# A delta-rule attention layer with a mixture of experts on one core: the 16-to-32 merge in 64x64 weights, and a new order of the work lists

## The chip, the cores and the metric

The kernel runs on one core of one Trainium2 chip. The metric is device time of one execution in microseconds (us), the median of the runs shown. A core has a matrix engine (PE, TensorE), a vector engine (DVE), a scalar engine (ACT), GpSimd (POOL) and a sync engine (SP) that only issues DMAs here. They work on 128 partitions of on-chip memory, each with its own instruction list, and meet at semaphores only.

## The reference, cut to what matters

```python
# x: (2, 2048, 128); 8 heads, key and value width 128
x = x + attention(layernorm(x))          # gated delta rule
x = x + moe(layernorm(x))                # 8 experts, the best 2 of each token

def step(S, inp):                        # inside attention, token by token
    q_t, k_t, v_t, beta_t, alpha_t = inp
    S = S * alpha_t
    kv = einsum('bhk,bhkv->bhv', k_t, S)
    S = S + einsum('bhk,bhv->bhkv', k_t, (v_t - kv) * beta_t)
    return S, einsum('bhk,bhkv->bhv', q_t, S)
```

q, k and v come from a projection and a causal convolution with four taps over time. The output is RMS-normalised per head, gated with silu(z), projected and added to x.

## The kernel before, in words

The 4096 tokens are 32 chunks of 128. Two chunks make a *group*; there are 16 groups. Inside a chunk the recurrence is solved with matrices: a lower triangular 128x128 matrix N per head and chunk (`Nm`) has to be turned into the inverse R of (1 + N), and then the chunk is a handful of 128x128 products.

The inverse is built bottom up. DVE inverts all 16x16 diagonal blocks by substitution (words `inv.0` to `inv.10`, lines 1055 to 1079; the blocks of a group lie one to a partition). They go out to DRAM (`to` on SP, `tp` on ACT) and come back as blocks on the diagonal of the 128x128 layout (`ti` on SP, line 508 for the tile `TA` and 511; `tj` on ACT, line 764). Then three merges double the block size. The first is the one that changes: `y16` (L1508) multiplies, for 16 head-chunks and 4 blocks of 32, a 32x32 weight of `Nm` by a 32x16 block of `TA`; ACT copies the result to `Y16` (`ye`, L807); `r16` (L1516) multiplies `Y16` by the other diagonal blocks; DVE negates the result into R (`re`, four instructions, L1209) and transposes the 32x32 blocks (`td`, L1218). The words `m.c.0` to `m.c.3` on PE with `me.c.0` to `me.c.3` on ACT are the merges to 64 and 128 (L1528 to L1564). After them `u.c.h` uses R.

All five lists come from one string, `ORDER`. Each engine walks the words from left to right and executes those that are its own; a word has a meaning in three pipelined stages: it *finishes* group g (merges, recurrence, output), it *prepares* group a = g+1 (projection, convolution, N, its inverse), and it *routes* the tokens of group g-1 to experts (words `sm s2 nr xt xe lg rk pf ps sc`). So the order of two words matters only where they are on the same engine. One pass over the string is called a period here. Words that come up below:

- 24 tiles of q, k and v: `proj.n` on PE (three matmuls, L1618 to L1620), `taps.n` on ACT (two instructions, L771), `first.n` on DVE (L1162, L1165), `last.n` on POOL (L650). The PSUM banks of `proj` are two: `proj.n` waits for `first.n-2`. The SBUF buffers are four: `taps.n` waits for `last.n-4`.
- `ka`, `aq` (POOL, L630), `diag` (POOL, L640), `scan` (DVE, L1173), `kk`, `kq`, `ktr` (PE, L1606, L1604), `nm`, `at` (DVE, L1183, L1193).
- `v`, `ks`, `u`, `sd`, `o` (PE, L1656, L1665, L1674, L1682, L1693), `rhs`, `ue`, `sq`, `kd` (ACT), `st`, `g`, `zg`, `x2` (DVE, L1225, L1236, L1199, L1243), `sp` (POOL, L662), `rms` (DVE), `gn`, `gte` (ACT, L856, L861), `gt`, `out` (PE, L1701, L1708).
- `rk`, `ps` (DVE) rank the experts and give each token a place; `sc` (POOL, L619) sends the rows of the group to their places with four indirect DMAs.

`y16` waits for the landing of all block DMAs (`t_in`). After the 16 groups the experts run over tiles of 256 rows; the diff does not touch that part.

## Time and profile before

| what | value |
|---|---|
| median of 3 runs | 1503.14 us (1501.5 to 1505.62) |
| profiled execution, its own time | 1506.71 us |
| its span, first to last instruction | 1504.6 us |
| PE busy, share of the span | 1171.7 us, 78% |
| PE weight loads | 1014.5 us, 67% |
| DVE | 1078.4 us, 72% |
| ACT | 926.1 us, 62% |
| POOL | 773.3 us, 51% |
| mean granted PE clock | 0.900 of full speed |
| chain of waits, share by engine | PE 37%, DVE 26%, issue 18%, ACT 8%, POOL 5% |

"Busy" is the time in which at least one instruction of the engine ran. "Issue" in the chain of waits is time in which an engine waited for nothing that the profile shows. A line of a timeline gives start, duration, engine, source line, operation, tiles, shape and count; in brackets the idle time of the engine before it and what ended it. A product of 32-bit numbers stands in the records as two MATMUL and two LDWEIGHTS, so 64 products of `y16` are 128 and 128 records. The first `y16` begins at 112.17 us, the last at 1202.23 us. The rest is the set-up before and the last group and the experts after.

### The profile page before, as it was taken

The numbers are of one execution on the slowest core, as the hardware profiler recorded it, in microseconds if no ns is written. First come the engines' busy times: TensorE is split into PE (matmuls) and PEld (weight loads), VectorE is DVE, ScalarE is ACT, GpSimd is POOL, SyncE is SP. The second block draws the span as 40 slices with busy tenths as digits, with TensorE's granted clock in tenths as the row PEclk, the third lists the DMA queues.
The fourth block names the chain that finished last, engine by engine and source line by source line (L and its number), as shares of the span: only waits on it lengthen the run. The fifth ranks groups of instructions, "written<-read, shape, count | busy, mean of one in ns | idle before, by whom it ended". The sixth has DMA issues, their size and how long they took to land.

```text
span 1504.6 us, 42594 instructions
## 1 busy us (share of the span) xinstructions
PE 1171.7 (78%) x15946; PEld 1014.5 (67%) x15946; DVE 1078.4 (72%) x2512; ACT 926.1 (62%) x2804; POOL 773.3 (51%) x723
## 2 busy tenths in 40 slices
PE   1478897979797979888888888888888875188881
PEld 1247786868686868777777777777877765176771
DVE  6686777777777777786868686868786914576664
ACT  1355775767576767676767676767575834166663
POOL 1237464646565565655555656474838332145452
PEclk9989998989798989898989999999998968599996
DMA  5132222221212121212121222222221241422214
GB/s 137 43 66 54 38 56 45 53 55 44 56 42 56 42 57 42 57 42 57 41 57 41 57 46 55 44 65 37 66 41 59 43 120 31 124 59 63 61 51 170
DMA packets 213501, 89.27 MB, mean 59 GB/s; under 512 B 167064, under 2 KB 200734, under 8 KB 212405
## 3 DMA queue, kind: packets, MB, share of 16 engines
q1 hardware_dynamic: 175220, 74.93, 19.8%
q0 software_dynamic: 4544, 8.47, 1.7%
q10 hardware_dynamic: 33536, 3.15, 1.6%
q8 instruction: 131, 2.15, 0.6%
q14 instruction: 70, 0.57, 0.1%
HBM read 65.72 MB, written 23.83 MB: 60 GB/s over the span
## 4 chain that ended last, share of the span: by engine, by line
PE 37%; DVE 26%; issue 18%; ACT 8%; POOL 5%; DMA 2%; SPq 1%; another core or an unknown queue 1%; POOLq 0%; DVEq 0%; ACTq 0%
DVE decay L1173 4%; DVE area L1165 3%; PE rc L1665 3%; PE ob L1694 3%; PE ob L1693 3%; DVE tapA L1162 2%; PE kx L1606 2%; PE ob L1508 2%; PE rc L1674 2%; PE pj L1618 2%; PE rc L1656 2%; DVE area L1183 2%; ACT Gs L856 2%; PE ob L1708 2%; ACT tapA L771 2%
## 5 line engine op out<-in xcount | busy, mean ns | idle before, releaser
L1162 DVE SCALAR_TENSOR_TENSOR tapA<-pj,taps,tapA 128x256 f32<-128x256 f32 x384 | 184.8, 481 | 221.3 <-ACT tapA L771 218.5
L650 POOL TENSOR_TENSOR kq<-tapA,area 128x256 f32<-128x256 f32 x256 | 243.9, 967 | 159.6 <-DVE area L1165 159.5
L771 ACT ACTIVATE area<-pj,taps 128x256 f32<-128x256 f32 x384 | 182.8, 476 | 219.8 <-PE pj L1620 172.7
L1165 DVE SCALAR_TENSOR_TENSOR area<-pj,taps,area 128x256 f32<-128x256 f32 x384 | 182.7, 476 | 0.0
L771 ACT ACTIVATE tapA<-pj,taps 128x256 f32<-128x256 f32 x384 | 181.8, 473 | 0.0
L650 POOL TENSOR_TENSOR vT<-tapA,area 128x256 f32<-128x256 f32 x128 | 92.0, 733 | 165.2 <-DVE area L1165 165.0
L1606 PE MATMUL kx<-kq 128*128 128x128 f32 x1024 | 148.3, 291 | 5.7 <-ACT GTs L861 4.6
L630 POOL TENSOR_TENSOR kq<-kq,area 128x1024 f32<-128x1024 f32 x64 | 150.1, 2356 | 0.0
L1606 PEld LDWEIGHTS kx<-kq 128*128 128x128 f32 x1024 | 134.9, 205 | 17.3 <-issue 14.6
L1618 PE MATMUL pj<-xn_hi,w_hi 128*128 128x259 f16 x384 | 118.4, 308 | 24.9 <-DVE area L1165 19.5
L679 POOL DMA_INDIRECT rows_out<-rhs,e_dst x78 | 82.8, 1061 | 91.4 <-ACT rhs L909 38.4
L662 POOL TENSOR_TENSOR S<-S,a_end 128x1024 f32<-128x1024 f32 x32 | 60.6, 1894 | 115.7 <-PE ob L1694 115.7
L1619 PE MATMUL pj<-xn_hi,w_lo 128*128 128x259 f16 x384 | 117.4, 306 | 0.0
L1620 PE MATMUL pj<-xn_lo,w_hi 128*128 128x259 f16 x384 | 116.9, 304 | 0.0
L1693 PE MATMUL ob<-S,kq 128*128 128x128 f32 x512 | 100.7, 279 | 0.0
L1694 PE MATMUL ob<-Us,area 128*128 128x128 f32 x512 | 99.7, 277 | 0.0
L1701 PE MATMUL kx<-ident,Gs 128*128 128x128 f32 x256 | 49.2, 338 | 60.9 <-ACT Gs L856 60.9
L1173 DVE TENSOR_TENSOR_SCAN decay<-area,decay 128x1024 f32<-128x1024 f32 x32 | 91.8, 2869 | 0.0
L619 POOL DMA_INDIRECT rows_in<-rowbuf,dest x64 | 63.8, 996 | 48.9 <-DVE dest L1151 32.9
L856 ACT ACTIVATE Gs<-Gs,rs 128x128 f32<-128x128 f32 x256 | 80.0, 395 | 13.4 <-DVE rs L240 13.4
L1701 PEld LDWEIGHTS kx<-ident,Gs 128*128 128x128 f32 x256 | 36.9, 173 | 71.7 <-ACT Gs L856 70.1
L1693 PEld LDWEIGHTS ob<-S,kq 128*128 128x128 f32 x512 | 80.0, 193 | 5.3 <-issue 2.9
(306 smaller groups left out, 3558.4 us busy)
## 6 DMA issues: line engine op xcount, KB each, us to landing
area<-scr_alpha SPq DMA_DIRECT2D x32, 512.0 KB
area<-scr_acum SPq DMA_DIRECT2D x32, 512.0 KB, 3.8
area<-rows_in SPq DMA_DIRECT2D x39, 130.0 KB
scr_n<-area SPq DMA_DIRECT2D x128, 32.0 KB, 1.7
area<-rows_out SPq DMA_DIRECT2D x4, 1024.0 KB, 8.0
rows_in<-rows_in SPq DMA_DIRECT2D x8, 260.0 KB
kq<-in_x SPq DMA_DIRECT2D x4, 512.0 KB, 6.1
blkN<-scr_n SPq DMA_DIRECT2D x32, 64.0 KB, 2.8
```

The costliest lines, as they stand in the source:

```text
L630: nc.gpsimd.tensor_tensor(t, t, acum_b[:, c, :, :], ALU.mult).then_inc(done, 1)
L650: nc.gpsimd.tensor_tensor(dst[:, n % H, :], tapA[:, n % RING, :], tapB[:, n % RING, :], ALU.add).then_inc(conv_done, 1)
L771: ins = nc.scalar.activation(dst[:, n % RING, :], pj[n % 2][:, k:k + GT], ACT.Copy, scale=taps[:, t, k:k + 1])
L1162: nc.vector.scalar_tensor_tensor(out=tapA[:, n % RING, :], in0=pj[n % 2][:, 0:GT], scalar=taps[:, order[n], 0:1], in1=tapA[:, n % RING, :] ...
L1165: nc.vector.scalar_tensor_tensor(out=tapB[:, n % RING, :], in0=pj[n % 2][:, 2:2 + GT], scalar=taps[:, order[n], 2:3], in1=tapB[:, n % RING ...
L1173: nc.vector.tensor_tensor_scan(decay[:, c, :, :].rearrange("p h c -> p (h c)"), alpha_b.rearrange("p h c -> p (h c)"), decay[:, c, :, :].r ...
L1606: ins = mm(o, lhs[:, hh, cs], rhs_[:, hh, cs], start=True, stop=True)
L1618: mm(o, wq_hi[:, w], xflat(xn_hi)[:, cols], start=True, stop=False)
L1619: mm(o, wq_lo[:, w], xflat(xn_hi)[:, cols], start=False, stop=False)
L1620: mm(o, wq_hi[:, w], xflat(xn_lo)[:, cols], start=False, stop=True).then_inc(proj_ready, 1)
L1693: mm(o, qT[1 - par][:, hh, C * c:C * c + C], S[:, c, hh, :], start=True, stop=False)
L1694: ins = mm(o, AT[:, c, hh, :], Us[:, hh, :], start=False, stop=True)
```

## The change

The 64 products of `y16` become 32, and those of `r16` as well. The four blocks of 32 are taken in pairs: the weight is the 64x64 diagonal block of `Nm`, the moving operand `T11` holds the 16x16 inverses of the two blocks side by side (64x32), and ACT writes four pieces into `Y16` in a block pattern over memory that was zeroed once (four instructions of 32 partitions where there was one of 128). `r16` multiplies a 64x64 weight of `Y16` by `R22` (64x16), a new tile that holds the lower 16x16 inverses; four more DMAs bring it. `r16` writes to bank `kx` 1 and no more to `ob` 1. `blkR` shares memory with `prod`. The word order is new throughout; no word is added or removed.

```diff
@@ sb tiles
-        blkR = sb("blkR", [128, SUB, SUB])
         prod = sb("prod", [128, 2 * (SUB - 1) * (SUB - 1)])
-        TA = sb("TA", [128, GC * H, SUB])
-        Y16 = sb("Y16", [128, GC * H, SUB])
+        blkR = prod[:, 0:SUB * SUB].rearrange("p (a b) -> p a b", b=SUB)
+        T11 = sb("T11", [128, GC * H, 2 * SUB])
+        Y16 = sb("Y16", [128, GC * H, 2 * BLK])
+        R22 = sb("R22", [128, GC * H, SUB])
@@ bank_of
-            if step in ("y16", "r16"):
+            if step == "y16":
                 return "ob", 1
+            if step == "r16":
+                return "kx", 1
@@ "ti" on SP
                         for b in range(NB):
-                            sp.dma_start(TA[BLK * b:BLK * b + SUB, :, :], a_blocks[b]).then_inc(t_in, 16)
+                            at = SUB * (b % 2)
+                            sp.dma_start(T11[BLK * b:BLK * b + SUB, :, at:at + SUB], a_blocks[b]).then_inc(t_in, 16)
+                            sp.dma_start(R22[BLK * b + SUB:BLK * b + BLK, :, :], r_blocks[b][SUB:BLK, :, SUB:BLK]).then_inc(t_in, 16)
@@ "ye" on ACT
-                        nc.scalar.activation(Y16.rearrange("p q j -> p (q j)"), ob[1][:, 0:GC * H * SUB], ACT.Copy).then_inc(y16_sb, 1)
+                        y = ob[1][:, :].rearrange("p (q j) -> p q j", j=2 * SUB)
+                        for b in range(NB):
+                            band, half_ = slice(BLK * b, BLK * b + BLK), b % 2
+                            ins = nc.scalar.activation(Y16[band, :, BLK * half_:BLK * half_ + SUB],
+                                                       y[band, :, SUB * half_:SUB * half_ + SUB], ACT.Copy)
+                        ins.then_inc(y16_sb, 1)
@@ "re" on DVE
-                                ob[1][top, GC * H * SUB:2 * GC * H * SUB].rearrange("p (q j) -> p q j", j=SUB), -1.0, ALU.mult)
+                                kx[1][top, 0:GC * H * SUB].rearrange("p (q j) -> p q j", j=SUB), -1.0, ALU.mult)
@@ small_blocks on PE
                 if step == "y16":
-                    pe.wait_ge(t_in, g * (32 * NB) + 32 * NB)
-                    y = ob[1][:, 0:n].rearrange("p (q j) -> p q j", j=SUB)
+                    pe.wait_ge(t_in, g * (48 * NB) + 48 * NB)
+                    y = ob[1][:, :].rearrange("p (q j) -> p q j", j=2 * SUB)
                     for q in range(GC * H):
-                        for b in range(NB):
-                            r_ = slice(BLK * b, BLK * b + BLK)
-                            ins = mm(y[r_, q], Nm[r_, q // H, q % H, r_], TA[r_, q, :], start=True, stop=True)
+                        for k in (slice(0, 64), slice(64, 128)):
+                            ins = mm(y[k, q], Nm[k, q // H, q % H, k], T11[k, q, :], start=True, stop=True)
                 else:
...
-                        for b in range(NB):
-                            r_ = slice(BLK * b, BLK * b + BLK)
-                            ins = mm(y[BLK * b:BLK * b + SUB, q], Y16[r_, q, :], Rq[r_, q, BLK * b + SUB:BLK * b + BLK], start=True, stop=True)
+                        for k in (slice(0, 64), slice(64, 128)):
+                            ins = mm(y[k, q], Y16[k, q, :], R22[k, q, :], start=True, stop=True)
```

The new order, split by engine, in the stretches that the prediction speaks of (from the period's first word up to `inv.0`, then the end):

```
PE   before  proj.0 y16 proj.1 r16 v.0.0 v.0.1 proj.2 proj.3 ks.0.0 m.1.0 m.0.0 ... proj.12 ktr.0.0 ktr.0.1 proj.13 v.1.1 u.1.0
     after   proj.0 proj.1 y16 proj.2 v.0.0 r16 proj.3 v.0.1 ks.0.0 proj.4 ks.0.1 m.1.0 m.0.0 ... sd.0.1 proj.12 proj.13 o.0.1
             proj.14 ktr.0.0 v.1.0 proj.15 v.1.1 ks.1.0
ACT  before  sm taps.0 ye taps.1 taps.2 ... taps.4 me.1.1 me.0.1 me.1.2 taps.5 ... sq.0.0 kd.0.0 taps.14 rhs.1.1 taps.15 ue.1.0
     after   taps.0 taps.1 ye taps.2 ... taps.5 me.1.1 me.0.1 me.1.2 taps.6 ... sq.0.0 taps.12 taps.13 taps.14 sq.0.1 taps.15
             rhs.1.0 rhs.1.1 scale.0 zt.0.0 ue.1.0 ue.1.1 kd.0.0
DVE  before  first.0 first.1 re td.0 ... first.4 first.5 first.6 first.7 scan.0 ... st.0.0 first.10 nm.0.1 scan.1 nm.1.0 nm.1.1
             first.11 first.12 st.0.1 first.13 g.0.0 first.14 first.15 inv.0
     after   first.0 first.1 first.2 re td.0 ... first.5 scan.0 first.6 ... nm.0.1 scan.1 nm.1.0 nm.1.1 first.10 first.11
             st.0.0 g.0.0 first.12 st.0.1 first.13 first.14 g.0.1 first.15 inv.0
POOL before  ka.0 last.0 last.1 aq.0 last.2 diag.0 last.3 diag.1 last.4 ... last.7 sp.0 ka.1 aq.1 last.8 last.9 last.10 last.11
     after   ka.0 last.0 aq.0 last.1 last.2 diag.0 last.3 ... last.7 diag.1 sp.0 last.8 aq.1 last.9 last.10 last.11 ka.1 last.12

the end of the period:
PE   before  z.1.1 gt.0.0 proj.16 gt.0.1 xt ... gt.1.0 gt.1.1 proj.21 kq.1.0 pf proj.22 out.1 proj.23 kq.1.1
     after   ... sd.1.1 kq.0.0 z.1.1 kq.0.1 proj.16 gt.0.0 ... gt.1.0 proj.20 pf proj.21 gt.1.1 kq.1.0 proj.22 kq.1.1 proj.23 out.1
ACT  before  ... gte.1.0 gte.1.1 taps.21 tj taps.22 taps.23
     after   ... gte.1.0 taps.20 taps.21 gte.1.1 tj taps.22 taps.23
DVE  before  ... rk first.20 x2.0 ps first.21 first.22 at.1.0 x2.1 first.23 at.1.1 st.1.1
     after   ... rk first.18 first.19 x2.0 ps first.20 first.21 st.1.0 at.1.0 first.22 first.23 x2.1 st.1.1 at.1.1
POOL before  nr last.16 ... last.20 sc last.21 last.22 last.23
     after   nr last.16 ... last.19 sc last.20 last.21 last.22 last.23
```

## Rows read from the trace of the kernel before

**Rows 1.** Windows, one period from `y16` to `y16` each: length, busy by engine, clock.

```profile
112.17:180.45 68.28, 60.17 (x880) 53.48 (x880) 51.53 (x113) 47.55 (x149) 37.71 (x32) 0.93 0.20 44
180.45:250.40 69.95, 60.00 (x893) 53.29 (x892) 56.31 (x127) 49.54 (x158) 38.94 (x35) 0.95 0.21 49
...
620.77:693.05 72.28, 62.73 (x892) 55.12 (x891) 56.31 (x127) 49.47 (x158) 42.88 (x40) 0.91 0.21 51
...
sum 1090.06, PE 933.37 PEld 820.08 DVE 838.40 ACT 740.95 POOL 633.59; mean PE 62.22 PEld 54.67 DVE 55.89 ACT 49.40 POOL 42.24
```

**Rows 2.** Waits of PE's weight loads, whole run: total us, times, longest.

```profile
PEld ob L1508 <- issue: 47.4, 74, 1.3
...
PEld ob L1516 <- issue: 25.8, 12, 5.0
```

**Rows 3.** Timeline of PE, `y16` of the eighth group (620.77).

```profile
620.77 0.45 PE L1508 MATMUL ob<-TA,area 32*32 32x16 f32 x33
...
624.67 1.38 PE L1508 MATMUL ob<-TA,area 32*32 32x16 f32 x85 [1.16 <-issue]
```

**Rows 4.** Timeline of PE, `y16` and `r16` of the second group (180.45).

```profile
180.45 1.26 PE L1508 MATMUL ob<-TA,area 32*32 32x16 f32 x128
...
185.53 1.07 PE L1516 MATMUL ob<-area,Y 32*16 32x16 f32 x109 [2.94 <-issue]
```

**Rows 5.** Timeline of POOL, first and last of the four indirect DMAs of one `sc`.

```profile
691.18 1.05 POOL L619 DMA_INDIRECT rows_in<-rowbuf,dest  x1 [1.18 <-DVE dest L1151]
...
695.09 0.97 POOL L619 DMA_INDIRECT rows_in<-rowbuf,dest  x1 [0.31 <-issue]
```

**Rows 6.** Timeline of DVE, idle before its line, and `scan.1`.

```profile
627.73 0.48 DVE L1162 SCALAR_TENSOR_TENSOR tapA<-pj,taps,tapA 128x256 f32<-128x256 f32 x1 [4.34 <-ACT tapA L771]
...
639.17 0.48 DVE L1162 SCALAR_TENSOR_TENSOR tapA<-pj,taps,tapA 128x256 f32<-128x256 f32 x1 [3.13 <-ACT tapA L771]
...
650.55 3.57 DVE L1173 TENSOR_TENSOR_SCAN decay<-area,decay 128x1024 f32<-128x1024 f32 x1
...
661.99 0.48 DVE L1162 SCALAR_TENSOR_TENSOR tapA<-pj,taps,tapA 128x256 f32<-128x256 f32 x1 [2.46 <-ACT tapA L771]
```

**Rows 7.** Windows: after `y16`'s gap; `m.1.0` to `inv.0`; `inv.0` to `y16`.

```profile
624.00:630.00 6.00, 5.33 (x226) 4.66 (x227) 2.20 (x6) 1.23 (x3) 6.00 (x7) 0.50 0.07 23
...
631.86:664.25 32.39, 29.98 (x419) 27.03 (x420) 22.78 (x39) 22.55 (x65) 21.21 (x16) 0.95 0.25 65
664.25:693.05 28.80, 24.61 (x193) 21.26 (x191) 26.93 (x75) 23.21 (x83) 11.21 (x15) 0.94 0.16 26
```

**Rows 8.** Timeline of PE, first and last of 32 records in two 64x64 quarters.

```profile
638.48 0.27 PE L1562 MATMUL ob<-T,area 64*64 64x64 f32 x1
...
639.41 0.22 PE L1564 MATMUL kx<-area 64*64 64x64 f32 x1
```

**Rows 9.** Timeline of PE: start of `m.1.0`, and two of its idle times.

```profile
631.86 0.18 PE L1414 MATMUL kx<-wab_hi 128*16 128x16 f16 x1 [0.26 <-DVE T L1218]
...
657.77 1.12 PE L1656 MATMUL rc<-ident,vT 128*128 128x128 f32 x4 [0.87 <-DVE S L1225]
...
677.37 0.70 PE L1701 MATMUL kx<-ident,Gs 128*128 128x128 f32 x4 [3.57 <-ACT Gs L856]
```

**Rows 10.** Timeline of ACT: `ye`, and `taps.12` held up by POOL.

```profile
626.09 0.38 ACT L807 ACTIVATE Y<-ob 128x256 f32<-128x256 f32 x1 [4.28 <-PE ob L1508]
...
654.74 0.47 ACT L771 ACTIVATE area<-pj,taps 128x256 f32<-128x256 f32 x1 [3.13 <-POOL kq L650]
```

**Rows 11.** The inverse's last instruction on DVE, and issues of `ti` and `tj`.

```profile
680.08 0.38 DVE L1069 COPY blkR<-blkT 128x256 f32<-128x256 f32 x1
...
684.59 1.78 SPq L508 DMA_DIRECT2D TA<-scr_a  x4
...
687.50 0.90 ACTq L764 DMA_DIRECT2D area<-scr_r  x2
```

**Rows 12.** DMA issues by line: count, KB, median us to landing.

```profile
area<-scr_r ACTq DMA_DIRECT2D x32, 64.0 KB, 2.5
```

45 lines of the change are left out of this document (22 added, 23 removed).

## The prediction, made before the changed kernel was run

> **What bounds the kernel now.** I read the windows first, one for each period [rows 1]. Fifteen periods make up 1090.06 us of the profiled execution's 1506.71 us; everything before and behind them the change leaves nearly alone. A period takes 72.67 us on average (1090.06 / 15), but PE is busy in 62.22 of them and DVE in 55.89: no engine is the bound by itself, the idle times are. So what counts is the few places where all engines stand at once.
>
> The waits of PE name the first place: the weight loads of `y16` waited 47.4 us in all, and those of `r16` 25.8 us, for nothing that the profile shows [rows 2]. The timeline shows how. In the eighth group `y16` begins at 620.77; 33 products' records pass at once, then come stalls of half a microsecond to 1.2 us with one to five records between them, and the last 85 pass from 624.67 on [rows 3]. It ends at 625.98, 5.2 us for work that took 1.26 us in the second group, where the 128 records came without a gap [rows 4]. While PE stands, `ye` waits 4.28 us on ACT [rows 10] and DVE is idle for 4.34 us [rows 6]; and PE goes on with a granted clock of 0.50, its lower level of 1.2 GHz, for six microseconds [rows 7].
>
> What the stalled groups have and the second hasn't is the `sc` of an earlier group: four indirect DMAs on POOL, from 691.18 to 696.06 (695.09 and 0.97) for the ninth group, whose `y16` begins at 693.05 [rows 5, 1]. That is a coincidence in time in all 14 groups from the third on, not a cause shown.
>
> The length of the periods prices the stall. The second period (180.45 to 250.40) has all of the later work, routing too, but no stall in its `y16`: 69.95 us. The 13 after it take (1090.06 - 68.28 - 69.95) / 13 = 73.22 us [rows 1]. The difference, 3.27 us, is close to the stall itself: it is on the path.
>
> The second place is `m.1.0` (631.86) to `inv.0` (664.25): 32.39 us with DVE busy in 22.8 [rows 7, 9]. Its two large holes are 3.13 us before 639.17 and 2.46 us before 661.99 [rows 6]. The third, `inv.0` to the next `y16`, is 28.80 us with DVE busy in 26.93: there DVE is the bound, though PE has a hole of 3.57 us before 677.37 in it [rows 7, 9].
>
> **The change part by part.**
>
> *`y16`, half the products.* 32 products are 64 MATMUL records. On half of the array each, 64x64 with 64 columns moved, 32 such records took 638.48 to 639.41, 0.93 us and one more step of 0.06, so two quarters in turn need about 31 ns for a record [rows 8]. 64 records are then 2.0 us at most; not under 0.5 x 1.26 = 0.63 us [rows 4]. I take 1.5 us, nearer to rows 8. So without a stall the products get no faster, 1.5 us for 1.26: what can go is the stall. Two things speak for that. Half the instructions pass the place at half the number a microsecond. And `y16` moves relative to `sc`: `ps`, which releases `sc`, comes one tile of DVE earlier (before `first.20`, not behind it), and `y16` waits for one tile more (`first.23`). A tile is two DVE instructions of 0.48 us that start 0.4 apart, 0.9 us [rows 6]. Today `y16` starts 1.9 us after `sc` does (693.05 - 691.18); it would start 3.7 us after, with 1.2 of the 4.9 us left [rows 5], and tiles 0 and 1 on ACT and DVE as cover. Bounds: 0 (it stays) to -3.7 us (5.2 - 1.5) in each of 14 groups. I take -3.2, the nearest to the 3.27 of rows 1.
>
> *`r16`.* Its stalls are 25.8 us over 15 periods, 1.7 each; in the second group 2.94 us stand after 19 records [rows 2, 4]. They are of another kind than those of `y16`: one long stall, also where no `sc` runs, as if the supply of instructions had run out. The two steps together have 128 MATMUL records and as many weight loads fewer to supply. Bounds 0 to -1.7, and the tile of 64 costs up to +0.7; I take -0.8.
>
> The Trainium skill ("Runtime: NRT & Kernel Launch", Instruction fetch mechanics) says that engines fetch instructions in blocks of 256 and that crossing a block is mostly hidden. By that rule the `r16` gaps would be something else and this term 0, the sum 12 us higher. The trace does not agree: 2.94 us were not hidden [rows 4].
>
> *The place of the two.* `y16` now stands behind `proj.1`, which waits for `first.23`, so the chain `y16`, `ye`, `r16`, `re`, `td`, `m.1.0` starts a tile of 0.9 us later [rows 6], and `ye` has four instructions for one of 0.38. `first.2` stands ahead of `re`, another 0.9 us if DVE isn't idle. Also `last.20` is now behind `sc`, and `taps.0` waits for it. Bounds 0 to +2.5, I take +1.0.
>
> *`m.1.0` to `inv.0`.* The hole of 3.13 us is the time in which ACT copies `me.1.1`, `me.0.1`, `me.1.2` and feeds no tile. DVE's `scan.0` moves from behind `first.7` to behind `first.5`, into the same hole: up to -3.1, if `diag.0` and the tile of alpha are there; POOL now does `diag.0` after `aq.0`, `last.1` and `last.2`. The hole of 2.46 comes from two hold-ups: `taps.12` stood 3.13 us for `last.8`, which was behind `ka.1` and `aq.1` [rows 10], and `v.1.1` stood 0.87 us for `st.0.1`, which was behind `scan.1` with its 3.57 us [rows 9, 6]. The new POOL list has `last.8` ahead of `aq.1` and `ka.1` behind `last.11`; PE gets `proj.12`, `proj.13` and `o.0.1` ahead of `v.1.0`. Bounds for both together 0 to -5.3; I take -2.5, about half, as no row tells what each engine would wait for next.
>
> *`inv.0` to `y16`.* No DVE work leaves this stretch, so closing PE's hole of 3.57 (with `kq.0.0`, `kq.0.1`, `proj.16`) gains little: 0. ACT loses cover: `rhs.1.0`, `rhs.1.1`, `ue.1.0` and `kd.0.0`, which it had done by 664.25, now come behind `taps.15`. That is about 3 us more in a stretch where ACT was busy for 23.21 of 28.80 us [rows 7]. It has 5.6 us of room, but in pieces. Bounds 0 to +3.0, I take +1.5.
>
> *The block DMAs.* Today the inverse ends at 680.46, `ti` issues from 684.59, six DMAs at 0.46 us, and `tj` issues at 687.50 and lands 0.90 + 2.5 us later at 690.9 [rows 11, 12]. `y16` comes 2.1 us after that. Four more issues on SP are +1.8 us: `ti` ends at 689.2 and lands by 691.6, still ahead. `gte.1.1` and with it `tj` move behind `pf` and `proj.21`. I take 0 and keep the other end for a rival.
>
> *Memsets* of two more tiles and the reuse of `prod` for `blkR`: once, or on DVE in its own order; 0.
>
> **The sum.** 14 x (-3.2) + 15 x (-0.8 + 1.0 - 2.5 + 1.5) = -44.8 - 12.0 = -56.8 us. Against the profiled execution's own 1506.71 this is 1449.9. The median of the runs is 3.6 us lower, 1503.14; so I forecast 1446 us. The forecast's own range, with the largest terms half way to one end or the other, is 1420 to 1470.
>
> **The rivals.**
>
> *The stall stays (0.18).* If it hangs on `sc` alone and the new place still overlaps it, 64 records are enough to run into it: the stall began after 33 records [rows 3]. Against: the shift of 1.8 us. Cover by tile 1 hides part, 1.0 us by the DVE tile of 0.9. 14 x 2.2 = +31: 1477 us.
>
> *The holes of `m.1.0` to `inv.0` close nearly to their end (0.12).* For it: DVE is idle for 9.6 us there (32.39 - 22.78) [rows 7] and the hold-ups on it are lifted one by one. 15 x (-5.3 + 2.5) = -42: 1404 us.
>
> *The wait for the landings takes the stall's place, and it is slower (0.12).* `gt.1.1` used to run ahead of `pf`, `tj` at 687.50. Now `pf` and `proj.21` come first and `taps.20`, `taps.21` are ahead of `gte.1.1` on ACT: `tj` moves back, by the 0.9 us of a tile for each of the three words that it is moved behind (2.7) and by up to 5.7 when ACT is behind by its +3.0; today's room is 2.1. PE would stand at the head of the period, with `proj.2`, `r16` and all merges queued behind it, and go on at clock 0.50 again, which costs as much as the stall. It decides from a landing 3.8 us behind `proj.1` on, the size of the forecast's gain in a period. At 5 us: 15 x 1.2 = +18, 1521 us. Against it: `proj.0` and `proj.1` wait for DVE too, and move `y16` back along with the landing.
>
> *The new order gives back what the stall gave (0.05).* +3.0 on ACT, nothing in the middle stretch: 1503 us, no change.
>
> **How the numbers follow.** The forecast has 0.50, and 0.03 lie between it and 1404. What a measurement can tell from no change is about 0.3%, 4.5 us. Faster: 0.50 + 0.18 + 0.12 + 0.03 = 0.83; same 0.05; slower 0.12. The range reaches over the staying stall to 1498 and over most of the third case to 1408.
>
> **What would show each step.** In the new profile: no "issue" before the new `y16` line beyond a few microseconds, and its 64 records in 1.5 us; periods of about 69 us; PE's clock at 1.00 behind it; DVE idle less than 1 us between `first.5` and `first.6`; no wait of `taps.12` for POOL. Wrong it would be if `y16` waits for a DMA, if the 3 to 4 us of stall are there with `sc` over by then, or if ACT is busy in over 26 us of the stretch from `inv.0`.

## The result, and the profile after

The changed kernel takes 1399.14 us (median of 3 runs, 1398.89 to 1415.56) against 1503.14: a ratio of 0.934, 95% interval 0.926 to 0.942. The direction was right; the time lies 47 us under the forecast of 1446 and 9 us under the range of 1408 to 1498. The profiled execution is the longest of them, 1415.56 us; it is 91 us shorter than that of before (1506.71), where 57 were forecast.

The page of the kernel after, busy time by engine and the chain of waits:

```profile
span 1413.4 us, 38612 instructions
...
PE 1191.2 (84%) x13898; PEld 1050.0 (74%) x13898; DVE 1042.3 (74%) x2512; ACT 935.2 (66%) x2852; POOL 773.3 (55%) x725
...
PE 53%; DVE 20%; ACT 10%; issue 9%; another core or an unknown queue 3%; POOL 2%; DMA 2%; SPq 1%; ACTq 0%; DVEq 0%; POOLq 0%
```

PE's share of the chain is 53% (37% before), issue has 9% (18%), DVE 20% (26%).

The windows of the periods, as in [rows 1]: second, eighth, and all fifteen.

```profile
180.64:245.55 64.91, 61.07 (x765) 55.14 (x764) 52.38 (x125) 49.95 (x159) 39.39 (x35) 0.95 0.24 55
...
587.39:656.48 69.09, 63.54 (x764) 56.76 (x763) 54.74 (x126) 50.05 (x159) 43.07 (x40) 0.93 0.23 54
...
sum 1018.35, PE 949.30 PEld 851.60 DVE 800.25 ACT 748.67 POOL 633.02; mean PE 63.29 PEld 56.77 DVE 53.35 ACT 49.91 POOL 42.20
```

The periods went from 1090.06 to 1018.35 us, 71.7 less. The rest is the tail, from the last `y16` to the experts: 109.0 us before, 87.8 after, 21.2 less. Set-up (112.2 to 114.1) and experts (193.4 to 193.1) hardly moved. 71.7 + 21.2 - 1.9 + 0.3 = 91.3 is the difference of the spans, within a tenth.

Each of the 14 periods from the second on, cut in three and summed by stretch. The first cut is the start of `m.1.0` on PE. The second, called `inv.0` below, is the first product of the inverse on DVE, which comes 0.5 us behind the first memset of `inv.0`, where [rows 7] cut (in h1 below, where a DMA is late, 1.0 us behind it). First before, then after: `y16` to `m.1.0`, `m.1.0` to `inv.0`, `inv.0` to `y16`.

```profile
sum 172.24, PE 117.47 PEld 97.55 DVE 99.63 ACT 52.02 POOL 143.38; mean PE 8.39 PEld 6.97 DVE 7.12 ACT 3.72 POOL 10.24
sum 449.04, PE 414.94 PEld 373.73 DVE 315.78 ACT 321.51 POOL 303.10; mean PE 29.64 PEld 26.70 DVE 22.56 ACT 22.96 POOL 21.65
sum 400.50, PE 340.79 PEld 295.31 DVE 371.46 ACT 319.88 POOL 149.41; mean PE 24.34 PEld 21.09 DVE 26.53 ACT 22.85 POOL 10.67
```

```profile
sum 167.73, PE 151.26 PEld 139.86 DVE 120.22 ACT 75.99 POOL 162.01; mean PE 10.80 PEld 9.99 DVE 8.59 ACT 5.43 POOL 11.57
sum 391.71, PE 380.09 PEld 342.10 DVE 291.82 ACT 299.60 POOL 304.96; mean PE 27.15 PEld 24.44 DVE 20.84 ACT 21.40 POOL 21.78
sum 392.36, PE 354.67 PEld 312.99 DVE 338.36 ACT 325.15 POOL 128.23; mean PE 25.33 PEld 22.36 DVE 24.17 ACT 23.23 POOL 9.16
```

Divided by 14, the stretches took 12.30, 32.07 and 28.61 us and take 11.98, 27.98 and 28.03. The first, where 3.7 us of stall a group went (59.0 / 16, see the waits below), is as long as it was: the new products and copies take longer, and DVE does 1.5 us more in it (7.12 to 8.59). The gain is in the middle one, where PE was busy in 29.64 of 32.07 us and is in 27.15 of 27.98.

PE's weight loads, as in [rows 2]; L1517 is `y16` now, L1523 `r16`:

```profile
PEld ob L1517 <- issue: 8.9, 24, 0.8
...
PEld kx L1523 <- issue: 5.3, 16, 1.1
```

The stalls are nearly gone: 47.4 to 8.9 us, and 25.8 to 5.3. Where a stall is given for one group from here on, it is the sum of the steps of over 0.12 us between the starts of the weight loads of `y16` or `r16`, on the mean of groups 3 to 16: `y16` 3.56 us before and 0.42 after, `r16` 1.62 and 0.

The work grew. PE in the eighth group (`y16`, `r16`), then ACT (`ye`); they answer to [rows 3, 4, 10]:

```profile
587.40 0.77 PE L1517 MATMUL ob<-T,area 64*64 64x32 f32 x20
588.62 1.49 PE L1517 MATMUL ob<-T,area 64*64 64x32 f32 x44 [0.45 <-issue]
...
591.95 2.83 PE L1523 MATMUL kx<-R,Y 64*64 64x16 f32 x64
```

```profile
590.17 1.52 ACT L816 ACTIVATE Y<-ob 32x256 f32<-32x256 f32 x4
```

44 records in 1.49 us are 34 ns each, where 128 passed in 1.26 us, 10 ns each [rows 4]. Half the products take 1.6 times the time (2.05 us in e2 below, where nothing stalls), and `ye` 1.52 us for 0.38.

`r16` also became sensitive to PE's clock. From its first record to the start of its last, its 64 records take 1.84 us where the granted clock is 1.00 (second and ninth group) and 3.34 us where it is 0.50 (twelfth and sixteenth). The 128 records of the old `r16` take 1.08 us at 0.50 (eighth and fourteenth group of before) and 1.05 at 1.00 (e1 below, fifth group). In the kernel after the mean granted clock during `r16` is between 0.50 and 0.83 in 14 of the 16 groups.

The tail: waits of the kernel before, then of the kernel after.

```profile
PEld kx L1576 <- POOL rowbuf L607: 23.1, 1, 23.1
...
ACT junk L736 <- DVE xres L1243: 14.6, 1, 14.6
...
DVE xres L1243 <- DMA xres<-in_x: 14.5, 1, 14.5
```

```profile
PEld kx L1583 <- POOL rowbuf L613: 10.0, 1, 10.0
...
ACT junk L742 <- DVE xres L1254: 1.0, 1, 1.0
```

Before, DVE waited once, 14.5 us, for a load of x. That is `xl.1` of the last group, which stood on SP behind `ti`, and there behind the eight copies that pad the experts' rows (issued from 1272.48 us on; the load follows at 1282.89). The new order has `xl.1` ahead of `to` and `ti`.

### The profile page after: what moved, and what is told of

The parts are those of the page before. It is cut to its first block, busy times and chain, and to the rows that moved or that the text cites. A ratio compares the mean times of both kernels' runs of the same rounds, so it can differ in the third digit from the quotient of the medians.

```text
span 1413.4 us, 38612 instructions
## 1 busy us (share of the span) xinstructions
PE 1191.2 (84%) x13898; PEld 1050.0 (74%) x13898; DVE 1042.3 (74%) x2512; ACT 935.2 (66%) x2852; POOL 773.3 (55%) x725
## 4 chain that ended last, share of the span: by engine, by line
PE 53%; DVE 20%; ACT 10%; issue 9%; another core or an unknown queue 3%; POOL 2%; DMA 2%; SPq 1%; ACTq 0%; DVEq 0%; POOLq 0%
PE rc L1672 5%; PE kx L1613 4%; PE ob L1700 3%; PE ob L1701 3%; PE kx L1523 3%; PE rc L1681 3%; DVE tapA L1173 3%; PE rc L1689 3%; PE pj L1625 3%; DVE area L1176 3%; PE rc L1663 2%; DVE decay L1184 2%; PE pj L1627 2%; ACT Gs L867 2%
## 5 line engine op out<-in xcount | busy, mean ns | idle before, releaser
L656 POOL TENSOR_TENSOR kq<-tapA,area 128x256 f32<-128x256 f32 x256 | 233.0, 917 | 168.3 <-DVE area L1176 167.2
L636 POOL TENSOR_TENSOR kq<-kq,area 128x1024 f32<-128x1024 f32 x64 | 162.7, 2543 | 0.0
L1625 PE MATMUL pj<-xn_hi,w_hi 128*128 128x259 f16 x384 | 114.6, 298 | 50.4 <-DVE area L1176 34.4
L1626 PE MATMUL pj<-xn_hi,w_lo 128*128 128x259 f16 x384 | 114.4, 298 | 0.0
L1625 PEld LDWEIGHTS pj<-xn_hi,w_hi 128*128 128x128 f16 x384 | 40.4, 105 | 77.3 <-DVE area L1176 48.8
L1184 DVE TENSOR_TENSOR_SCAN decay<-area,decay 128x1024 f32<-128x1024 f32 x32 | 86.7, 2710 | 0.0
L858 ACT ACTIVATE area<-ob 128x128 f32<-128x128 f32 x256 | 67.8, 292 | 25.7 <-PE ob L1701 25.7
L610 POOL TENSOR_TENSOR rowbuf<-rowbuf,id_step 128x4 int32<-128x4 int32 x16 | 3.2, 199 | 145.7 <-DVE rs L241 145.7
L1672 PE MATMUL rc<-S,kq 128*128 128x128 f32 x512 | 82.7, 322 | 0.0
```

The costliest lines, as they stand in the source:

```text
L636: nc.gpsimd.tensor_tensor(t, t, acum_b[:, c, :, :], ALU.mult).then_inc(done, 1)
L656: nc.gpsimd.tensor_tensor(dst[:, n % H, :], tapA[:, n % RING, :], tapB[:, n % RING, :], ALU.add).then_inc(conv_done, 1)
L1184: nc.vector.tensor_tensor_scan(decay[:, c, :, :].rearrange("p h c -> p (h c)"), alpha_b.rearrange("p h c -> p (h c)"), decay[:, c, :, :].r ...
L1625: mm(o, wq_hi[:, w], xflat(xn_hi)[:, cols], start=True, stop=False)
L1672: ins = mm(heads(rc[u])[:, h, :], kT[1 - par][:, hh, C * c:C * c + C], S[:, c, hh, :], start=False, stop=(h == HU - 1))
```

## The experiments

Each was timed in five rounds (the first four in three) against the kernel before in the same series, and all ratios are to it. The kernel before took 1450 us in the first series, 1503, 1500 and 1507 in the next three, 1453 in the last: the level of the series changes, so times are compared within one only. Period: mean of the 15. The stretches are means of the 14 from the second on, each from one profiled execution; the tail as above. The profile of f1 is of one of its longer executions (1408.74 us; they took 1387.7 to 1410.09), so differences of a few tenths of a us in a period against it mean nothing. "Before" and "after" in the first two lines are the profiles already shown.

| kernel | ratio, 95% interval | period | y16 to m.1.0 | m.1.0 to inv.0 | inv.0 to y16 | tail |
|---|---|---|---|---|---|---|
| before | 1 | 72.67 | 12.30 | 32.07 | 28.61 | 109.0 |
| after | 0.934 [0.926, 0.942] | 67.89 | 11.98 | 27.98 | 28.03 | 87.8 |
| series 1: e1, new order alone | 0.924 [0.920, 0.928] | 65.18 | 10.53 | 27.86 | 26.93 | 87.6 |
| e2, new products alone | 1.003 [1.000, 1.007] | 71.80 | 10.71 | 32.67 | 28.50 | 103.4 |
| e3, xl.1 ahead | 0.990 [0.985, 0.995] | 71.43 | 10.82 | 32.18 | 28.43 | 92.6 |
| e4, sc later | 0.995 [0.993, 0.998] | 71.99 | 10.46 | 33.21 | 28.43 | 102.8 |
| series 2: f1, full change | 0.933 [0.927, 0.939] | 67.57 | 12.10 | 27.78 | 27.91 | 87.6 |
| f2, new order alone | 0.923 [0.919, 0.928] | 66.81 | 10.36 | 28.45 | 28.35 | 85.9 |
| g1, new up to inv.0 | 1.028 [1.024, 1.032] | 74.78 | 13.28 | 33.85 | 27.84 | 103.2 |
| g2, old up to inv.0 | 0.995 [0.992, 0.998] | 72.80 | 12.66 | 33.47 | 27.00 | 91.1 |
| series 3: h1, chunk 1 behind tile 15, old order | 1.033 [1.030, 1.036] | 75.59 | 12.16 | 31.03 | 32.50 | 107.8 |
| h4, chunk 1 ahead, new order | 1.037 [1.032, 1.042] | 75.80 | 12.54 | 35.61 | 27.85 | 91.8 |
| h2, POOL's old list | 0.944 [0.939, 0.948] | 67.40 | 12.50 | 27.58 | 27.42 | 95.0 |
| h3, xl.1 back | 0.943 [0.940, 0.946] | 66.71 | 11.36 | 27.37 | 28.02 | 98.7 |
| series 4: i1, old start, new rest | 0.955 [0.951, 0.959] | 69.48 | 12.98 | 29.67 | 27.03 | 85.1 |
| i2, new up to tile 15 | 1.003 [1.000, 1.005] | 72.73 | 13.77 | 28.12 | 31.00 | 108.1 |
| i3, kq behind gt.0.0 | 0.992 [0.989, 0.996] | 72.24 | 10.72 | 28.40 | 33.58 | 93.9 |
| i4, new order, sc later | 0.943 [0.939, 0.946] | 67.79 | 9.39 | 30.89 | 27.70 | 91.3 |
| series 5: j1, sc later again | 0.997 [0.995, 1.000] | 71.70 | 10.65 | 32.95 | 28.34 | 100.6 |
| j2, the kernel before | 1.001 [0.998, 1.003] | 71.73 | 11.00 | 32.60 | 28.39 | 105.7 |

### The two halves of the change

`e1_order_only` has the products of before in the new order:

```diff
-        ORDER = """ (list of before) """
+        ORDER = """ (list of after) """
```

> The kernel before with the new word order alone; the products of y16 and r16 stay 64 each in 32x32 weights, and r16 stays in bank ob 1. Theory A (the order is most of the gain, the halving little: the new place of y16 behind sc takes most of the stall away): about 1410 to 1425 us, the y16 of groups 3 to 16 in under 3 us. Theory B (the halving is the larger part, as the prediction had it: -45 us for y16 and -12 for r16): the stall of 3.7 us stays in y16, and the time is 1440 to 1460.

`e2_products_only` is the counterpart: everything of the diff but `ORDER`.

> The new kernel with the old word order: only the 64x64 products, the four copies and the four more DMAs. Theory A (the stall hangs on sc at the same time, whatever the products): y16 still takes about 5 us, 64 records or not, and the time is within 1495 to 1515. Theory B (fewer instructions take the stall away): y16 in 1.5 to 2.5 us from the third group on, periods of 70 us, 1450 to 1465 us.

The order is the whole gain, the products are none of it: 0.924 and 1.003. e2 has no stall over 0.12 us inside any `y16` or `r16`, and its period is 71.80 us. But PE stands 1.3 us in front of each `r16`, for the four copies of `ye`: the new products trade stalls for work. One thing is not covered: in this series the kernel before takes 1450 us, and at that level its `y16` stalls only 0.63 us (j2 below), not 3.56. What the products alone give where `y16` stalls 3.56 us was not run.

The order alone and the full change were run again side by side, in a series where the kernel before takes 1503 us:

> The changed kernel itself, on one chip with the kernel before and with the three next kernels, because the first pair of times came from another chip than the four experiments did. If chips differ only in the stage of the experts and in small stalls, its ratio to the kernel before is near that of the new order alone (0.924) plus the 0.3% that the new products cost in the old order: 0.927. If the 64x64 products cost more inside the new order, because no stall is left for them to remove, its ratio is 0.934 as on the first chip.

> The products of before in the new order, a second time, beside the full change. Theory: the whole gain is the order's, so this is 0.924 of the kernel before again, and 0.3% under the full change or level with it. Rival: the products carry part of the gain, and the full change is ahead of it by 0.5% or more.

The full change gives 0.933 and the order alone 0.923, medians of 1407.36 and 1390.26 us in the same series. The quotient of the two ratios is 1.011, interval 1.002 to 1.019 (both errors in quadrature): the 64x64 products cost about 1% inside the new order. f2 beats both kernels. Its two steps and its `ye` in the eighth group, on PE and ACT:

```profile
581.04 0.67 PE L1506 MATMUL ob<-TA,area 32*32 32x16 f32 x22
582.22 1.18 PE L1506 MATMUL ob<-TA,area 32*32 32x16 f32 x106 [0.52 <-issue]
...
585.54 1.22 PE L1514 MATMUL ob<-area,Y 32*16 32x16 f32 x128
```

```profile
583.76 0.40 ACT L805 ACTIVATE Y<-ob 128x256 f32<-128x256 f32 x1
```

`r16` follows `y16` at 4.5 us (585.54 - 581.04), in the full change at 4.55 (591.95 - 587.40), but it is done in 1.22 us instead of 2.83. `y16` to `m.1.0` is 10.36 us instead of 12.10; 1.1 of that is given back in the other two stretches.

### The stall of `y16`

`e4_sc_later` and `j1_sc_later` take `sc` away from `y16`:

```diff
                 for step, *arg in STEPS:
-                    if r is not None:
+                    if r is not None and (step != "sc" or a is None):
                         route(step, r, par)
+                    if step == "last" and arg == [2] and g is not None and g >= 2:
+                        route("sc", g - 2, 1 - par)
```

> The kernel before with sc (the four indirect DMAs on POOL) moved into the next period, ahead of last.2, some ten microseconds later. Theory A (the stall of y16 is caused by sc): y16 takes 1.3 us in all groups, and stalls of 0.7 us show in the small products that now stand beside sc (merges to 64, L1528 to L1541). Theory B (the stall belongs to y16 and its place in the instruction stream): y16 still takes 5 us. The time: A 1470 to 1500 as POOL holds last.2 up by 5 us and the merges may stall instead; B 1505 to 1530.

> The kernel before with sc issued behind last.2 of the next period, a second time, beside the kernel before with its own profile: in the series of the first time (where the kernel before took 1450 us) no profile of it was taken, and another kernel of the old order showed stalls of y16 of only 0.55 us. My prediction's term: the stall of 3.5 us is on the path at 3.2 us a group, so without it the kernel is 14 x 3.2 = 45 us faster: ratio 0.970. Theory now: the stall is only moved, to r16 (2.9 us there the first time), and POOL comes late by sc's 4.9 us with ka and aq; 1 us a period at most: ratio 0.99 to 1.00.

> The kernel before itself: its ratio has to be 1 within 0.3 to 0.4%, which shows what a comparison of this kind can tell. Its profile gives the stalls of y16 and r16 and the three stretches of a period in the same series as the run above: 3.5 and 1.7 us as on the first chip if the kernel takes 1500 us; 0.5 and 2.5 us if it takes 1450.

In e4 no `y16` of any group stalls for more than 0.3 us, and in j1 only those of the tenth and the fifteenth do. So without `sc` beside it this stall goes; `r16` stalls 2.8 to 2.9 us, and the kernel gains 0.5% the first time and 0.3% the second. The waits of PE's weight loads in j2, the kernel before, in a series in which it takes 1453 us (L1516 is `r16`, L1508 `y16`):

```profile
PEld ob L1516 <- issue: 40.1, 19, 3.4
...
PEld ob L1508 <- issue: 9.0, 35, 1.4
```

`y16`'s stalls are 9.0 us here, not 47.4, and `r16`'s 40.1, not 25.8 [rows 2]. `sc` runs beside `y16` in j2 exactly as it did (it starts 1.9 us before it and ends 3.0 us behind its start, in both profiles). So `sc` is needed for the stall but doesn't set its size: 0.63 us a group here, 3.56 in the first profile, in the same kernel. And e4 and j1 took away the small stall only; against j2, `y16` loses 0.5 us in j1 and `r16` gains 0.3 (2.56 to 2.82).

The same kernel at both levels gives a rough price. `y16` stands 2.9 us a group less in j2 (3.56 to 0.63), `r16` 0.9 more (1.62 to 2.56), and the period is 0.94 us shorter, `y16` to `m.1.0` 1.3. If the 0.9 of `r16` cost nothing, 2.9 us of stall were worth 1.3; if they cost their full length, 2.2. My estimate from these numbers is 1.6 to 2.7 us for 3.56, not 3.2. It rests on two profiles from different series.

`i4_order_sc_later` is the same edit in the new order, with the old products.

> A version that may beat both kernels: the products of before, the new order throughout, and sc of a group issued behind last.2 of the next period, so that no indirect DMA of POOL stands beside y16. Theory: the stalls of y16 (1.2 us a period there) go, but those of r16 grow or are hidden; ratio 0.915 to 0.923, against 0.923 without the move. Rival: POOL comes late with ka and aq for the first chunk, the stretch behind m.1.0 grows, and the ratio is 0.93 or more.

The rival came in. `y16` to `m.1.0` is the shortest of all, 9.39 us, and `m.1.0` to `inv.0` 2.4 us longer than in f2: POOL is busy in 25.85 us of that stretch for 23.27, and 0.923 becomes 0.943. Both kernels ran where the kernel before takes 1500 us, so here the move meets a larger stall: `y16` goes from 1.18 us a group in f2 to 0.24, and `r16` from 0.63 to 1.51. `sc` apart from `y16` helps `y16` at both levels, and `r16` stalls more.

The stalls of `r16` have a cause of their own. The profile lists the packets of a queue of kind "instruction", 16 KiB each. First before, then after:

```profile
q8 instruction: 131, 2.15, 0.6%
q8 instruction: 115, 1.88, 0.6%
```

These are PE's instructions: the change removes 4096 of PE's records (2048 MATMUL and 2048 LDWEIGHTS) and 16 packets, so a packet is 256 of them. And the stalls of `r16` hang on them. In the second group of before the packet ends at 184.07 us and the stall at 185.53 [rows 4], 1.46 us later. The ten profiles with the old products have 131 gaps of over 0.4 us between two weight loads of one `r16`, and every one ends 0.97 to 1.62 us after such a packet has ended, though the packets come several us apart. So `r16` waits there for its own instructions. The repeated gaps of 0.6 us in `y16`, beside `sc`, have no such distance to a packet. None of the ten profiles with the new products has a gap of that kind in `r16`.

### The load of x

`e3_xl_ahead` moves one word in the old order, `h3_xl_back` moves it back in the new one:

```diff
-  SP:  ... bi to ti xl.1 xs.0 xs.1
+  SP:  ... bi xl.1 to ti xs.0 xs.1
```

> The kernel before with one word moved on SP: xl.1 stands ahead of to and ti. In the last group ti is followed by the eight fills of rows_in, which wait for the last place table; xl.1 stood behind them. Theory A (that is where 14.5 us of the tail went): 1486 to 1491 us, and x2.1 of the last group waits for no DMA. Theory B (the tail is bound by the last recurrence anyway): within 1499 to 1505.

> The full change with xl.1 (the load of x's second chunk on SP) back behind ti. Theory: before the experts, the load stands behind ti and the eight copies of the padding again, and the tail from the last y16 to the experts is 10 to 20 us longer (87.6 us now, 103 to 109 before): ratio 0.941 to 0.947, periods unchanged at 67.6 us. Rival: in the periods too DVE's x2.1 waits for it, +0.5 us each, and the ratio is above 0.95; or the tail came from elsewhere and nothing changes.

Ahead, the tail is 92.6 us (105.7 in j2, at the same level); back, 98.7 (87.6 in f1). So this word is 11 to 13 of the tail's 21 us, and about 1% of the time both ways (0.990; 0.933 to 0.943, which spans two series). h3's waits show the load again:

```profile
DVE xres L1252 <- DMA xres<-in_x: 13.5, 1, 13.5
```

`h2_pool_old` gives POOL its list of before in the full change.

> The full change with POOL's old list: aq.1 and ka.1 ahead of last.8, last.1 ahead of aq.0, diag.1 ahead of last.4, sc behind last.20. Theory (PE bounds the middle stretch): ACT waits up to 3 us for last.8, as before, but most of it lies beside PE's work: period +0.5 us or less, ratio 0.933 to 0.938. Rival, as my prediction had it: the hold-up of 3.13 us before taps.12 was on the path and most of it comes back, +2 us a period or more, ratio 0.953 or above.

0.944, between the two numbers expected, and for a reason that neither named. The period is unchanged (67.40 us), but this doesn't price the hold-up of `last.8` behind `ka.1` and `aq.1`: it didn't come back. ACT waits for POOL's `last` in 2.8 us of the whole run here, and did in 44.4 before; the new lists of the other engines are enough to hide it. The tail is 7.4 us longer: PE's one wait for `rowbuf` (POOL) is 17.8 us, 10.0 in f1. What in POOL's list does it was not separated.

### Where in the period

`g1_new_to_inv` and `g2_old_to_inv` join the halves of the two lists at `inv.0`.

> The new products; every list in the new order up to inv.0 and, for the words that are left, in the old order behind it (xl.1 stays behind ti on SP). Theory: the gain of a period is made between m.1.0 and inv.0, 4.1 of 4.8 us on the first chip (32.07 to 27.98 us). Then the period falls from 71.8 us to 67.8 or less, and the tail stays at 103 us: 1450 - 15 x 4 = 1390, ratio 0.958. Rival: the order of the end of the period has to go with it, since what is pulled ahead of inv.0 is paid for behind it; then the stretch from inv.0 to y16 gets longer, the period falls by 2 us or less, and the ratio is 0.98 or more.

> The counterpart: the old order of every list up to inv.0, the new order of what is left behind it, xl.1 ahead of to and ti on SP, the new products. Theory: behind inv.0 the new order gives 0.6 us a period at most, and xl.1 about 11 us in the tail: 1454 - 9 - 11 = 1434, ratio 0.989. Rival: the end of the period carries the gain, the period falls by 2 us or more, and the ratio is 0.97 or less.

Both theories fell. g1 is 2.8% slower than before, and its middle stretch, which has the new order, is 33.85 us. g2 gains no more than `xl.1` brings. In g1 the cut at `inv.0` leaves `v.1.0`, `ks.1.0`, `ktr.0.0`, `ktr.0.1`, `v.1.1`, `u.1.0`, `ks.1.1`, the start of the second chunk, in front of and among `proj.12` to `proj.15` on PE; the new order has only `ktr.0.0` and `v.1.0` there. Two kernels move just these words.

```diff
h1, in the old order:
-  PE:  ... kk.1.0 v.1.0 ks.1.0 kk.1.1 sd.0.1 proj.12 ktr.0.0 ktr.0.1 proj.13 v.1.1 u.1.0 proj.14 ks.1.1 proj.15 o.0.1
+  PE:  ... kk.1.0 kk.1.1 sd.0.1 proj.12 proj.13 proj.14 proj.15 ktr.0.0 v.1.0 v.1.1 ks.1.0 ktr.0.1 ks.1.1 u.1.0 o.0.1
-  ACT: scale.0 taps.12 rhs.1.0 taps.13 sq.0.0 kd.0.0 taps.14 rhs.1.1 taps.15 ue.1.0
+  ACT: scale.0 taps.12 taps.13 sq.0.0 taps.14 taps.15 rhs.1.0 rhs.1.1 kd.0.0 ue.1.0
h4, in the full change:
-  PE:  sd.0.1 proj.12 proj.13 o.0.1 proj.14 ktr.0.0 v.1.0 proj.15 v.1.1 ks.1.0 ks.1.1
+  PE:  sd.0.1 v.1.0 ks.1.0 proj.12 ktr.0.0 ktr.0.1 proj.13 v.1.1 o.0.1 proj.14 ks.1.1 proj.15
```

> The kernel before with one part of the new order: PE does ktr.0.0, v.1.0, v.1.1, ks.1.0, ktr.0.1, ks.1.1 and u.1.0, the start of the second chunk's recurrence, behind proj.15 instead of between the projections, and ACT does rhs.1.0, rhs.1.1, kd.0.0 and ue.1.0 behind taps.15. Theory: PE is the bound of the stretch from m.1.0 to inv.0 (busy in 29.6 of 32.07 us there before, 27.0 of 27.8 after), and the gain comes from work that leaves it for the stretch of the inverse, where PE is busy in 24.3 of 28.6. Seven words are about 7 us of PE (8 records of 1.0 to 1.9 us each for a word of ks, some 2 for v), of which part sits there in both orders: the middle stretch falls by 3 us or more, the end stretch grows by less than 1, the period falls by 2.5 and the ratio is 0.975. Rival: the middle is bound by the chain through ACT and POOL (last.8 behind ka.1 and aq.1), and nothing comes of it: ratio 0.995 to 1.01.

> The counterpart, in the full change and on PE alone: v.1.0, ks.1.0, ktr.0.1, v.1.1 and ks.1.1 go back among proj.12 to proj.15, as in the order of before; all other lists are the new ones. Theory (PE bounds the middle stretch): what is put back there delays proj.15 and with it inv.0; four words of 1 to 2 us, so the middle stretch grows by 3 us or more and the ratio goes from 0.933 to 0.965 or above. Rival: DVE and ACT set the end of the stretch, PE has room, and the ratio stays below 0.94.

h1 misses both expectations: the middle stretch is 1.0 us shorter, the end 3.9 longer, 1.033. Its middle and its end, summed over the 14 periods:

```profile
sum 434.37, PE 363.86 PEld 319.22 DVE 315.03 ACT 276.16 POOL 295.75; mean PE 25.99 PEld 22.80 DVE 22.50 ACT 19.73 POOL 21.12
sum 454.99, PE 417.02 PEld 371.48 DVE 348.31 ACT 362.84 POOL 155.18; mean PE 29.79 PEld 26.53 DVE 24.88 ACT 25.92 POOL 11.08
```

3.6 us of PE's work left the middle (29.64 to 25.99), and it became 1.0 us shorter. So PE's work alone doesn't bound the old middle, though it fills 92% of it. In the end it took 5.5 us more and made it 3.9 longer. (Cut at the first memset of `inv.0`, the middle is 1.6 us shorter and the end 4.4 longer, as DVE waits there for the blocks.)

h4 comes as the theory said, 1.037, but is no clean proof of it: PE's `ks.1.0` now waits for `ka.1`, which POOL has in its new place behind `last.11`.

```profile
PEld rc L1671 <- POOL kq L635: 38.7, 15, 3.2
```

38.7 us over 15 periods are 2.6 of the 7.8 that its middle stretch grew. What both show is that, of the two places tried, each order is faster with its own.

`i1_old_start` (products of before) keeps the old order up to `m.1.0` only; `i2_new_to_tile15` has the new order up to tile 15, PE's words included, and the old end (one word of POOL departs from this: `ka.1` stands behind `last.8`, not behind `last.11`).

```diff
i1, against the new order (ACT and POOL likewise, and xl.0 on SP):
-  PE:  proj.0 proj.1 y16 proj.2 v.0.0 r16 proj.3 v.0.1 ks.0.0 proj.4 ks.0.1 m.1.0
+  PE:  proj.0 y16 proj.1 r16 v.0.0 v.0.1 proj.2 proj.3 ks.0.0 proj.4 ks.0.1 m.1.0
-  DVE: first.0 first.1 first.2 re td.0 first.3 td.1
+  DVE: first.0 first.1 re td.0 first.2 td.1 first.3
```

> The products of before; the old order up to m.1.0 (y16 and r16 early, re ahead of first.2, sm first on ACT) and the new order from there on. So it differs from the kernel with the new order throughout (0.923) in the start alone. Theory: the start carries the gain. From y16 to m.1.0 takes as long after as before (12.2 and 12.5 us), but DVE has done first.4 by then (11.9) where it had only done first.2; the two tiles more are worth 2.2 us each, and with the old start they are lost: first.8 comes at 26 us or later instead of 22.6, the period grows by 3 to 4 us, ratio 0.955 to 0.965. Rival: the stretch behind m.1.0 carries it, and the ratio stays below 0.94.

> The new products; the new order up to tile 15 on every engine (PE too, with only ktr.0.0 and v.1.0 of the second chunk ahead of proj.15), the old order of what is left behind it, xl.1 behind ti. Theory: the first part keeps its gain of 4.5 us (inv.0 at 40 us after y16 instead of 44.6), but the second chunk's chain now starts late and the old end has no place for it: inverse to y16 takes 31 to 33 us instead of 28.6, as with that chain moved alone, and the ratio is 0.99 to 1.01. Rival: the first part carries the gain by itself, the end stays near 28.6, and the ratio is 0.955 or less.

Both ratios are where the theory had them, 0.955 and 1.003. The start is worth 2.7 us a period (66.81 in f2 to 69.48), nearly half of the order's 5.9 (72.67 to 66.81); part of that may be stall, as `y16` and `r16` together stall 3.7 us a group in i1 and 1.8 in f2. What it does is seen on DVE between `y16` and `m.1.0` in the eighth group, first before (620.77 to 631.86), then after (587.40 to 600.11):

```profile
622.52 0.48 DVE L1162 SCALAR_TENSOR_TENSOR tapA<-pj,taps,tapA 128x256 f32<-128x256 f32 x1
...
628.63 1.72 DVE L1209 TENSOR_SCALAR area<-ob 16x256 f32<-16x256 f32 x4
...
631.84 0.48 DVE L1162 SCALAR_TENSOR_TENSOR tapA<-pj,taps,tapA 128x256 f32<-128x256 f32 x1
```

```profile
590.93 0.48 DVE L1173 SCALAR_TENSOR_TENSOR tapA<-pj,taps,tapA 128x256 f32<-128x256 f32 x1
...
592.59 0.48 DVE L1173 SCALAR_TENSOR_TENSOR tapA<-pj,taps,tapA 128x256 f32<-128x256 f32 x1 [0.78 <-ACT tapA L777]
...
594.83 1.72 DVE L1220 TENSOR_SCALAR area<-kx 16x256 f32<-16x256 f32 x4 [1.36 <-PE kx L1523]
...
598.03 0.48 DVE L1173 SCALAR_TENSOR_TENSOR tapA<-pj,taps,tapA 128x256 f32<-128x256 f32 x1
...
599.67 0.48 DVE L1173 SCALAR_TENSOR_TENSOR tapA<-pj,taps,tapA 128x256 f32<-128x256 f32 x1
```

`first.0` and `first.1` come before the `re` in both (622.52 with 627.73 [rows 6]; 590.15 and 590.93). But before, `first.2` begins at 631.84, with `m.1.0`; after, `first.2` has its place ahead of `re` at 592.59, and `first.3` and `first.4` come before `m.1.0` too. Two tiles more are done while the chain `y16`, `ye`, `r16`, `re`, `td` runs. On the mean of groups 3 to 15 `first.5` begins 15.4 us after `y16` instead of 20.2.

i2 keeps the middle (28.12 us for 27.78 in f1) and pays in the end, 31.00 for 27.91:

```profile
sum 393.69, PE 377.32 PEld 340.40 DVE 288.59 ACT 305.35 POOL 308.88; mean PE 26.95 PEld 24.31 DVE 20.61 ACT 21.81 POOL 22.06
sum 434.08, PE 373.04 PEld 321.52 DVE 353.78 ACT 329.28 POOL 111.34; mean PE 26.65 PEld 22.97 DVE 25.27 ACT 23.52 POOL 7.95
```

`i3_kq_back` undoes one move of the end:

```diff
-  PE:  z.1.0 sd.1.1 kq.0.0 z.1.1 kq.0.1 proj.16 gt.0.0 proj.17 xt gt.0.1 lg proj.18 proj.19
+  PE:  z.1.0 sd.1.1 z.1.1 gt.0.0 proj.16 proj.17 kq.0.0 xt gt.0.1 lg proj.18 kq.0.1 proj.19
-  DVE: g.1.1 at.0.0 inv.9 zg.1.1 at.0.1 inv.10 first.16 first.17 rk first.18 first.19
+  DVE: g.1.1 inv.9 zg.1.1 inv.10 first.16 first.17 at.0.0 rk first.18 at.0.1 first.19
```

> The full change with kq.0.0, kq.0.1 and proj.16 back behind gt.0.0 on PE, and at.0.0 and at.0.1 behind first.17 and first.18 on DVE, as before. My prediction priced this move at 0, because DVE is the bound of the end. Theory: the end holds the second chunk's chain only because gt.0.0 and the tiles 16 and up don't stand behind one another; undone, PE stands for gte.0.0 again with the tiles queued behind it, 2 to 3.5 us a period, ratio 0.955 to 0.985. Rival (the prediction's term): within 0.5 us a period, ratio 0.933 to 0.940.

0.992, more than the theory had: the end grows from 27.91 to 33.58 us, the period from 67.57 to 72.24. PE in the eighth period has a hole before `gt.0.0` again, and one before `xt` (L1582):

```profile
666.28 0.66 PE L1707 MATMUL kx<-ident,Gs 128*128 128x128 f32 x4 [1.79 <-ACT Gs L866]
...
671.52 0.41 PE L1582 MATMUL kx<-ident,rowbuf 128*128 128x128 f32 x2 [1.89 <-DVE area L1203]
```

The edit moves two words of DVE as well, so the 5.7 us are those of the group of five words and not of PE's hole alone: `xt` waits for `at.0.0` (L1203), which comes late.

## Why the prediction was wrong, point by point

**"Everything before and behind [the periods] the change leaves nearly alone."** This step failed: it put the tail at nothing, and the tail fell by 21.2 us. With them the sum would have been 1429 against the profiled 1415.6; and without them the measured 1399 would be 1420, inside the range. The wait of 14.5 us stood in the waits of the trace of before, and the diff moves the word behind it, `xl.1`. I read only the part of the trace that repeats. h3 and e3 show that this word is 11 to 13 us of it; POOL's new list is 7.4 (h2).

**The price of `y16`'s stall, 3.2 us in 14 groups.** The largest term, and wrong in size. That the stall would go was right (47.4 to 8.9 us of waits), and so was the shift behind `sc`: `y16` starts 3.8 to 5.1 us after it now, 3.7 were forecast. That it hangs on `sc` was right too, but `sc` alone doesn't set its length (j2). The price came from the second period, which has no stall in `y16` and is 3.27 us shorter than the later ones. One period is no yardstick: in e2, which has no stall inside either step, the second is 2.4 us shorter than the later ones too (69.7; 72.0 on average), in e4 it is 0.9 longer (72.9; 72.0). It may be short for the 4 us of POOL that it lacks (38.94 us busy, 42.88 in the eighth [rows 1]). By the estimate above the stall was worth 22 to 38 us in 14 groups, not 44.8. And the first stretch, where the stall was, got no shorter: the new work of `y16`, `ye` and `r16` took its place.

**The products in 1.5 us.** I had 31 ns a record from [rows 8], 2.0 us, and then took 1.5, between that and the lower bound, with no row for it. From its first record to the start of its last, `y16` takes 2.26 us on average with 0.4 of stall in it. `r16` has 2.61 for 2.77, hardly faster though its stalls went, since its records now slow down with the clock: the sign that I had named, PE's clock at 1.00 behind `y16`, did not come. `ye` is +1.14. So the first stretch gave 0.32 us where the terms -3.2, -0.8 and +1.0 said 3.0.

What the stalls of `r16` cost by themselves stays open. e2 and j2 look like the pair to read: 2.6 us a group in j2, none in e2, periods of 71.73 and 71.80 us. But from the start of `y16` to the end of `r16` they take 6.3 us in j2 and 6.4 in e2, as e2's longer copies and products fill what the stalls left.

The Trainium skill ("Runtime: NRT & Kernel Launch", Instruction fetch mechanics) has the crossing of an instruction block mostly hidden. The trace agrees for most blocks: before has 131 packets and 12 such gaps in `r16`. Those in `r16` were what the forecast took them for, a supply of instructions that had run out; that they would vanish with half the records was right.

That the kernel without this half is the faster one (f2) was none of my cases: I took the products to be the cause of the gain.

**`m.1.0` to `inv.0`, -2.5 us.** Measured -4.10. The step counted DVE's holes, and half of them. What the two hold-ups that it named are worth was not measured; POOL's is gone from the waits (44.4 us before), and stays gone with POOL's old list (h2). The step left out two things. Two tiles are done before the stretch: with the old start it is 1.2 us longer (i1 against f2). And the second chunk's words have left it, so that PE has 2.5 us less to do there; that this shortens it is argued, not shown, as h1 and h4 moved those words in orders where other engines waited for them.

**`inv.0` to `y16`, +1.5 us.** Measured -0.58. The cost on ACT didn't come: its busy time there rose by 0.4 us (22.85 to 23.23), where about 3 were expected. And "closing PE's hole gains little: 0", since DVE is the bound, failed: with the five words moved back the stretch is 5.7 us longer and the period 4.7 (i3).

**The block DMAs at 0** was right; the rival with the landing did not come. No `y16` waits longer than a few tenths for them (1.4 us in 16 groups), though 192 DMAs brought them instead of 128.

Together: 44.8 + 12.0 forecast for the periods, 71.7 measured, so the sum of the periods came near by luck. Its terms for the first stretch said 3.0 us a group and it gave 0.32; its terms for the other two said 1.0 and they gave 4.7. Over 14 groups the first is some 38 us too large, the other some 51 too small, and the two errors hide each other but for the 15 us that are left. The last 13 us of the miss are the medians: the profiled execution of after lies 16.4 us over its median, that of before 3.6.

What stays open: which word of POOL's list lengthens the tail; how much of the middle stretch each of its moves gives, since no half of the order could be tried without breaking into the other; how much of the order's gain is the stall that it takes away (5.2 us a group before, `y16` and `r16` together, 1.8 in f2); what makes the stall of `y16` 3.56 us in one profile and 0.63 in another; what the products alone do where it is 3.56; and what sets the level of a series. It is not the chip alone: the record gives chip 6 for the series at 1450 us and for those at 1503 and 1500.
